# Second cross-attention with precomputed key maps, values as the stationary operand, and exponentials that take the maximum as their bias

## The chip, the cores and the metric

The kernel runs on one core of a Trainium2 chip. The time is device microseconds of one execution, median of three runs. The engines are TensorE (PE in the profile; its weight loads are PEld), VectorE (DVE), ScalarE (ACT), GpSimd (POOL) and SyncE (SP), each with its own instruction stream; they meet by semaphores.

## What is computed

Two layers, each a cross-attention with residual and a mixture-of-experts feed-forward with residual, over x of 8 images x 128 tokens x 128, all in float32. The context has 77 rows of 96 for each image. The change touches the second attention, which has 16 heads of 64:

```python
q = (layernorm(x) @ Wq).reshape(B, Nq, 16, 64)      # Wq 128 x 1024
k = (context @ Wk).reshape(B, Nk, 16, 64)           # Nk = 77
v = (context @ Wv).reshape(B, Nk, 16, 64)
attn = softmax(einsum('bqhd,bkhd->bhqk', q, k) / 8)
x = x + einsum('bhqk,bkhd->bqhd', attn, v).reshape(B, Nq, 1024) @ Wo + bo
```

Ahead of it stand the first attention (16 heads of 8) and the first expert layer (16 experts, 4 for each token); behind it the second expert layer (8 experts, one for each token).

## The kernel before

Each engine has a stream written out by hand, the order of which nothing alters. PSUM has eight banks, named S0 to S3, T0, T1, O and M. `plan_banks` writes down the order in which each bank is filled and emptied, and every user waits on the bank's `filled` or `freed` semaphore. An "image" below is one b of the eight. The stages in time are the first attention (to 109 us), routing and the first expert loop `fixed_units` (to 188), the second attention (`attention_1`, to 353), routing tables, and the second expert loop `units_1`.

In the second attention TensorE does for each image:
- `xT`: transposes the normalised tokens (ScalarE copies them to XT1);
- `q`: 8 matmuls of 128 columns give the queries of all heads, in two halves, copied to QT1 by ScalarE;
- `scores`: 16 matmuls of 77 columns on 64 rows each, two heads on two row halves;
- `probsT`: 16 transposes of the exponentials, four heads (a group g) in one bank; ScalarE copies them to PT;
- `pv`: 16 matmuls with the transposed exponentials stationary and the values moving, 65 columns each; the 65th column is of ones and gives the sum;
- `outT`: 8 transposes of the normalised result OS; ScalarE copies them to OT;
- `proj`: 8 matmuls of 128 columns, accumulated;
- `xnT`, `logits`, `rank`: the routing of an earlier image.

VectorE does for each group of four heads `shift` (maximum over the keys, then an addition that writes the shifted scores to SBUF) and `pv_out` (reciprocal of the sums, multiplication into OS). ScalarE's `exps` runs one exponential of 308 columns a group, in place. For each image VectorE has further `combine` (the sum of the four gathered expert rows and the statistics for the norm), `attn_norm`, `proj_out`, `normed`, and the small steps of the routing `choose`, `place` and `gate_out`. GpSimd gathers the expert rows of the first layer (`gather`, four indirect DMAs an image, three images ahead), raises variances to a power (`ln_pow` for the norm ahead of attention, `route_rstd` for the one ahead of routing), scatters routed tokens (`scatter`) and their row words (`meta`).

Keys K1 of the second layer are made during the first attention, all values V1 at the entry of the second (`v1`, 16 matmuls of 512 columns), 12 of them ahead of the first `xT`. SyncE loads the expert weights of the second layer into W, one expert after each image's scores.

## Time and profile before

| | us |
|---|---|
| median of 3 runs | 408.42 (405.4 to 409.94) |
| the profiled execution, its own time | 410.49 |
| its span, first to last instruction | 408.7 |
| TensorE busy | 353.8 (87%) |
| VectorE busy | 201.5 (49%) |
| ScalarE busy | 156.7 (38%) |
| GpSimd busy | 131.4 (32%) |
| mean granted clock of TensorE | 0.818 |

The span is the profiled execution's stretch from the first instruction to the last, 1.8 us less than that execution's time. Busy times count instructions that overlap once.
### The profile page before, as it was taken

How to read it: one execution, taken by the hardware profiler on the slowest of the kernel's cores; microseconds unless marked ns; L12 is line 12 of the kernel's file. 1: busy time of each engine (PE TensorE's matmuls, PEld its weight loads, DVE VectorE, ACT ScalarE, POOL GpSimd, SP SyncE). 2: the span in 40 equal slices, each digit the busy share in tenths (PEclk: the TensorE clock that was granted, in tenths of full speed). 3: DMA queues.
4: the chain of work that ended last, by engine and by line, in shares of the span. 5: the costliest groups of instructions: out<-in, count | busy, mean ns of one | idle time of the engine just before them, and what ended most of it. 6: DMA issues, size and time to landing. Idle time of an engine off the chain costs nothing.

```text
span 408.7 us, 8350 instructions
## 1 busy us (share of the span) xinstructions
PE 353.8 (87%) x2925; PEld 287.5 (70%) x2934; DVE 201.5 (49%) x697; ACT 156.7 (38%) x392; POOL 131.4 (32%) x192
## 2 busy tenths in 40 slices
PE   7789998998887799999987997969699999679990
PEld 4456675676664698985556996959599888549980
DVE  4455433443244566772268365535346663325760
ACT  1643202221243477666553343232215333015650
POOL 6314235423554000002764023412403203252441
PEclk9999558566586899998998599876859989559997
DMA  7999500000813567861132012120020210028711
GB/s 182 326 284 281 174 27 27 14 14 28 290 66 88 169 191 224 227 176 58 51 98 84 8 60 67 38 61 18 26 60 7 67 60 7 9 55 268 234 55 64
DMA packets 43545, 43.38 MB, mean 106 GB/s; under 512 B 6496, under 2 KB 39504, under 8 KB 43488
## 3 DMA queue, kind: packets, MB, share of 16 engines
q1 hardware_dynamic: 35488, 32.21, 27.3%
q0 software_dynamic: 3040, 5.74, 4.7%
q10 hardware_dynamic: 4976, 4.90, 3.7%
q8 instruction: 24, 0.39, 0.4%
q14 instruction: 17, 0.14, 0.1%
HBM read 26.29 MB, written 17.07 MB: 106 GB/s over the span
## 4 chain that ended last, share of the span: by engine, by line
PE 64%; issue 11%; DVE 5%; another core or an unknown queue 4%; SPq 4%; DMA 4%; ACT 4%; POOL 1%; POOLq 0%; ACTq 0%; DVEq 0%
PE bank_S L1949 6%; PE bank_M L1704 5%; PE bank_M L1678 4%; PE bank_O L1632 4%; PE bank_T L1661 3%; PE bank_S L1588 3%; PE bank_M L1742 3%; PE bank_S L1650 3%; PE bank_O L1678 3%; PE bank_O L1626 3%; PE bank_S L2003 3%; PE bank_S L1602 2%; PE bank_O L1958 2%; PE bank_M L1958 2%
## 5 line engine op out<-in xcount | busy, mean ns | idle before, releaser
L750 POOL DMA_INDIRECT dispatched<-XN,slot_u x40 | 40.2, 1004 | 22.5 <-DVE slot_u L1257 13.2
L758 POOL DMA_INDIRECT G<-expert_out,yslot x32 | 31.0, 969 | 19.5 <-DMA expert_out<-OS 10.6
L836 ACT ACTIVATE PT<-bank_T 77x512 f32<-77x512 f32 x40 | 23.0, 590 | 26.0 <-PE bank_T L1661 24.7
L734 POOL TENSOR_SCALAR var_eps<-row_data 128x1 f32<-128x1 f32 x8 | 1.8, 225 | 82.6 <-DVE row_data L1109 82.6
L836 ACT ACTIVATE QT<-bank_T 128x256 f32<-128x256 f32 (+2 forms) x47 | 16.5, 352 | 29.1 <-PE bank_T L1970 8.2
L879 ACT ACTIVATE scratch<-scratch 128x308 f32<-128x308 f32 x32 | 14.6, 457 | 30.5 <-DVE scratch L1169 27.0
L1678 PE MATMUL bank_M<-late,PT 77*128 77x65 f32 x112 | 18.1, 312 | 9.0 <-ACT QT L836 9.0
L1190 DVE RECIPROCAL RS<-bank_O 128x128 f32<-128x128 f32 x8 | 7.7, 957 | 34.1 <-PE bank_O L1632 18.2
L1704 PE MATMUL bank_M<-Wo_sb,OT 128*128 128x128 f32 x128 | 23.2, 356 | 0.8 <-ACT OT L836 0.8
L1678 PEld LDWEIGHTS bank_M<-late,PT 77*128 77x128 f32 x112 | 16.2, 223 | 10.6 <-ACT QT L836 9.7
L1163 DVE TENSOR_REDUCE negmax<-bank_S 128x4 f32<-128x308 f32 x32 | 15.1, 473 | 16.4 <-PE bank_S L1650 13.1
L1661 PE MATMUL bank_T<-C,scratch 128*77 128x128 f32 x128 | 22.5, 310 | 0.0
L1704 PEld LDWEIGHTS bank_M<-Wo_sb,OT 128*128 128x128 f32 x128 | 21.7, 264 | 1.0 <-issue 1.0
L1678 PE MATMUL bank_O<-late,PT 77*128 77x65 f32 x112 | 17.5, 307 | 4.5 <-DVE lg L1222 3.9
L820 POOL DMA_INDIRECT result<-OS,token x15 | 14.4, 957 | 19.0 <-DVE OS L1504 17.5
L1650 PE MATMUL bank_S<-K,QT 64*128 64x77 f32 x256 | 20.3, 306 | 0.0
L1678 PEld LDWEIGHTS bank_O<-late,PT 77*128 77x128 f32 x112 | 16.0, 221 | 5.9 <-DVE lg L1222 4.3
L836 ACT ACTIVATE QT<-bank_M 128x512 f32<-128x512 f32 x13 | 7.8, 597 | 30.7 <-remote 16.7
L1650 PEld LDWEIGHTS bank_S<-K,QT 64*128 64x128 f32 x256 | 17.9, 213 | 2.1 <-issue 0.8
L728 POOL TENSOR_SCALAR var_eps<-mv 128x1 f32<-128x1 f32 x8 | 2.1, 264 | 52.7 <-DVE mv L1109 52.7
L783 POOL TENSOR_TENSOR late<-late,C 128x1 f32<-128x1 f32 x15 | 3.1, 205 | 49.4 <-DMA late<-wp_dram 49.4
L1661 PEld LDWEIGHTS bank_T<-C,scratch 128*77 128x77 f32 x128 | 17.8, 175 | 1.1 <-issue 1.1
(286 smaller groups left out, 911.1 us busy)
## 6 DMA issues: line engine op xcount, KB each, us to landing
dispatched<-zeros SPq DMA_DIRECT2D x8, 1024.0 KB, 9.5
...
```

The costliest lines, as they stand in the source:

```text
L750: nc.gpsimd.indirect_dma_start(out=xs_dram, out_offset=bass.IndirectOffsetOnAxis(ap=slot_u[:, b, k:k + 1], axis=0), in_=XN[:, b, :], in_of ...
L758: nc.gpsimd.indirect_dma_start(out=G[:, b % 2, k, :], out_offset=None, in_=ys_dram, in_offset=bass.IndirectOffsetOnAxis(ap=yslot[:, b, k:k ...
L836: nc.scalar.activation(dst, src, func, **kw).then_inc(freed[bk], 1)
L879: nc.scalar.activation(pg, pg, ACT.Exp, scale=float(HD[1]) ** -0.5).then_inc(exp_done, 1)
L1163: link(nc.vector.tensor_reduce(negmax[:, g, :], sc, AX_X, ALU.max, negate=True))
L1632: ins = nc.tensor.matmul(bank["O"][32 * g:32 * g + 32, 128:256], C[0:M, C_SUM + 32 * j:C_SUM + 32 * j + 32], PT0[b % 2][:, g, 128 * j:128 ...
L1650: ins = nc.tensor.matmul(bank[f"S{g0 + k}"][:, M * j:M * j + M], QT1[r, b % 2, 2 * g0 + j, :], K1[r, 2 * g0 + j, M * b:M * b + M], start=T ...
L1661: ins = nc.tensor.transpose(o[0:M, 128 * j:128 * j + 128], P[:, b % 2, g, M * j:M * j + M], ident)
L1678: ins = nc.tensor.matmul(bank[bk][:, d * j:d * j + d], PT[:, g, 128 * j:128 * j + 128], V1[:, b, head_at(g, j), :], start=True, stop=True)
L1704: ins = nc.tensor.matmul(o[:, 0:128], OT[:, c, :], Wo_sb[:, c, :], start=(c == 0), stop=(c == 7))
L1949: nc.tensor.matmul(o[:, 0:256], weights_of(u)[:, 128 * half:128 * half + 128], xeT[:, r:r + 2, :], start=True, stop=True).then_inc(filled[ ...
L1958: ins = nc.tensor.matmul(o[:, 128 * m:128 * m + 128], hs[:, 2 * (u % RING) + m, :], weights_of(u)[:, 256:384], start=True, stop=True)
```

## The change

The scores of head h are X Wq_h K_h^T, so Wq_h K_h^T can be made without the tokens. `maps` does this at the entry: for 8 pairs of heads and two halves of four images, 32 matmuls of 308 columns on 64 rows each, into A1, which lies over W. `q` and its copies go; `scores` becomes 4 matmuls of 308 columns on all 128 rows. The factor 1/8 moves into the copies of K1.

`pv` has the values stationary (64 columns) and the transposed probabilities moving (128 columns); two heads write the two partition halves of a bank, which is already the form `proj` wants, so `outT`, OS and the 65th column go. Since the rows can't be scaled behind it any more, the probabilities are scaled ahead of the transposes: `scaled` on VectorE takes sums, reciprocal and product over 8 heads (616 columns). ScalarE's `exps` reads PSUM with the negative maximum as its bias, which makes 16 activations of 77 columns out of 4 of 308. VectorE's maxima are taken over 616 columns, two an image.

The order of all five streams is written anew: routing of an image stands one image later on VectorE, GpSimd's `ln_pow` stands between pairs of gathers, and the row words of the early images are sent near the end.

```diff
+        W = sb("W", [128, B * NH * M])
+        A1 = W[:].rearrange("p (b h m) -> p b h m", b=B, h=NH)
...
             ln_pow(0)
...
             gather(1, (2, 3))
-            gather(2)
+            gather(2, (0, 1))
             ln_pow(1)
-            for b in range(B - 1):
+            gather(2, (2, 3))
+            for b in range(B):
                 if b + 3 < B:
-                    gather(b + 3)
+                    gather(b + 3, (0, 1))
                 if b + 2 < B:
                     ln_pow(b + 2)
+                if b + 3 < B:
+                    gather(b + 3, (2, 3))
                 if 0 <= b - 1:
                     route_rstd(1, b - 1)
-                if 0 <= b - 2:
-                    scatter(1, b - 2)
...
+                if b == 6:
                     pool.wait_ge(meta_zeroed, 16)
-                if 0 <= b - 3:
-                    meta(b - 3)
-            route_rstd(1, B - 2)
+                    meta(0)
+                    meta(1)
...
             def exps(b, g):
-                act.wait_ge(freed[f"S{g}"], J(f"S{g}", "scores", 1, b, g))
-                pg = P[:, b % 2, g, :]
-                nc.scalar.activation(pg, pg, ACT.Exp, scale=float(HD[1]) ** -0.5).then_inc(exp_done, 1)
+                act.wait_ge(max_ready, 2 * b + g // 2 + 1)
+                tb = f"T{g % 2}"
+                if b >= 2:
+                    act.wait_ge(filled[tb], J(tb, "pT", 1, b - 2, g))
+                else:
+                    act.wait_ge(filled["O"], J("O", "u", 0, B - 1, 0))
+                for j in range(GH):
+                    ins = nc.scalar.activation(P[:, b % 2, g, M * j:M * j + M], bank[f"S{g}"][:, M * j:M * j + M], ACT.Exp,
+                                               bias=negmax[:, g, j:j + 1])
+                ins.then_inc(freed[f"S{g}"], 1)
...
+            def map_out(half):
+                for c in range(8):
+                    bk = map_bank(c, 0)
+                    copy_out(bk, J(bk, "map", half, c, 0), A1[:, 4 * half:4 * half + 4, 2 * c, :],
+                             bank[bk][:, 0:308].rearrange("p (b m) -> p b m", b=4))
...
+            def maxima_1(b, n):
+
+                if b > 0:
+                    for g in (2 * n, 2 * n + 1):
+                        dve.wait_ge(freed[f"S{g}"], J(f"S{g}", "scores", 1, b - 1, g))
+                for g in (2 * n, 2 * n + 1):
+                    dve.wait_ge(filled[f"S{g}"], J(f"S{g}", "scores", 1, b, g))
+                nc.vector.tensor_reduce(negmax[:, 2 * n:2 * n + 2, :],
+                                        bank_S[:, 2 * n:2 * n + 2, 0:GM].rearrange("p g (h m) -> p g h m", h=GH),
+                                        AX_X, ALU.max, negate=True).then_inc(max_ready, 1)
+
+            def scaled(b, n):
+
+                for g in (2 * n, 2 * n + 1):
+                    dve.wait_ge(freed[f"S{g}"], J(f"S{g}", "scores", 1, b, g))
+                pg = P[:, b % 2, 2 * n:2 * n + 2, :].rearrange("p g (h m) -> p (g h) m", h=GH)
+                link(nc.vector.tensor_reduce(psum[:, 2 * n:2 * n + 2, :].rearrange("p g h -> p (g h)"), pg, AX_X, ALU.add))
+                link(nc.vector.reciprocal(recip[:, 2 * n:2 * n + 2, :], psum[:, 2 * n:2 * n + 2, :]))
+                r = recip[:, 2 * n:2 * n + 2, :].rearrange("p g h -> p (g h)")
+                nc.vector.tensor_tensor(pg, pg, r[:, :, None].to_broadcast([128, 2 * GH, M]), ALU.mult).then_inc(p_ready, 1)
...
-                shift(0, 1)
+                maxima_1(0, 0)
+                maxima_1(0, 1)
+                v1_out(10)
                 combine(1)
...
+                scaled(0, 0)
+                v1_out(12)
...
+                maxima_1(1, 1)
+                scaled(1, 0)
+                for b in range(1, B):
+                    scaled(b, 1)
+                    if b + 1 < B:
+                        maxima_1(b + 1, 0)
+                    if 0 <= b - 3:
+                        choose(1, b - 3)
                     if b + 2 < B:
                         combine(b + 2)
-                    pv_out(b, 0)
-                    shift(b + 1, 0)
-                    shift(b + 1, 1)
-                    pv_out(b, 1)
-                    shift(b + 1, 2)
-                    pv_out(b, 2)
+                    proj_out(1, b - 1)
+                    if b + 1 < B:
+                        maxima_1(b + 1, 1)
                     if 0 <= b - 3:
...
+                        place(1, b - 3)
                     if b + 2 < B:
                         attn_norm(b + 2)
...
+                    if b + 1 < B:
+                        scaled(b + 1, 0)
+                    normed(1, b - 1)
+                    if 0 <= b - 4:
+                        gate_out(b - 4, b - 3)
...
             dve.wait_ge(ld_c, LD_C)
+            map_out(0)
+            v1_out(1)
+            v1_out(3)
+            map_out(1)
+            v1_out(5)
+            v1_out(7)
+            v1_out(9)
             combine(0)
             attn_norm(0)
...
+            def maps(half):
...
+                for c in range(8):
+                    for k in range(2):
+                        bk = map_bank(c, k)
+                        o = use(bk, J(bk, "map", half, c, k))
+                        r = slice(64 * k, 64 * k + 64)
+                        nc.tensor.matmul(o[:, 0:308], Wq_sb[r, c, :], K1[r, c, 308 * half:308 * half + 308],
+                                         start=True, stop=True).then_inc(filled[bk], 1)
...
+            def scores(b, n):
+                if n == 0:
+                    pe.wait_ge(freed["T0"], J("T0", "xT", b))
...
+                for g in (2 * n, 2 * n + 1):
+                    o = use(f"S{g}", J(f"S{g}", "scores", 1, b, g))
+                    nc.tensor.matmul(o[:, 0:GM], XT1[:], A1[:, b, GH * g:GH * g + GH, :], start=True, stop=True)\
+                        .then_inc(filled[f"S{g}"], 1)
...
-                pe.wait_ge(exp_done, NG * b + g + 1)
+                pe.wait_ge(p_ready, 2 * b + g // 2 + 1)
...
+            def pv(b, n):
+                bk, number = product("pv", 1, b, n)
                 o = use(bk, number)
+                for m in (2 * b, 2 * b + 1):
+                    pe.wait_ge(freed[v1_bank(m)], J(v1_bank(m), "v1", m))
...
+                    pe.wait_ge(freed[f"T{g % 2}"], J(f"T{g % 2}", "pT", 1, b, g))
                 for c in range(4):
...
+                    for k in range(2):
+                        h = 8 * n + 2 * c + k
+                        j = h % GH
+                        ins = nc.tensor.matmul(o[64 * k:64 * k + 64, 128 * c:128 * c + 128], V1[:, b, h, :],
+                                               PT[:, h // GH, 128 * j:128 * j + 128], start=True, stop=True)
                 ins.then_inc(filled[bk], 1)
...
+                maps(0)
+                v1(0, 4)
+                maps(1)
+                v1(4, 6)
+                xT(0)
+                scores(0, 0)
+                scores(0, 1)
+                v1(10, 4)
...
                 probsT(0, 0)
...
+                for b in range(1, B):
+                    if b + 1 < B:
+                        scores(b + 1, 0)
                     probsT(b, 0)
-                    xT(b + 1)
                     probsT(b, 1)
-                    if last:
-                        outT(b - 1, 0)
-                    q(b + 1, 0)
+                    proj(1, b - 1)
                     pv(b, 0)
-                    scores(b + 1, (0, 1))
-                    q(b + 1, 1)
+                    if b + 1 < B:
+                        scores(b + 1, 1)
+                    if 0 <= b - 3:
+                        rank(1, b - 3)
                     probsT(b, 2)
-                    if last:
-                        outT(b - 1, 1)
+                    probsT(b, 3)
+                    if 0 <= b - 2:
+                        xnT(1, b - 2)
+                    if b + 2 < B:
+                        xT(b + 2)
                     pv(b, 1)
-                    probsT(b, 3)
-                    if routed:
-                        xnT(1, b - 2)
-                    scores(b + 1, (2, 3))
-                    pv(b, 2)
-                    if routed:
+                    if 0 <= b - 2:
                         logits(1, b - 2)
```

The maps at the entry. TensorE, from the last matmuls of `fixed_units`, before (L1912 and L1958 are the expert loop's, L2003 is `v1`, L1734 `xT`, L1742 `q`, L1650 `scores`):

```order
L1912 MATMUL bank_T<-b_sb,OT 128x128 x4
L1958 MATMUL bank_O<-late,OS 128x128 x2
L2003 MATMUL bank_S<-Wv_sb,ctx_sb 77x512 x12
L1734 MATMUL bank_M<-C,XA 128x128
L1742 MATMUL bank_M<-XT,Wq_sb 128x128 x4
L1742 MATMUL bank_O<-XT,Wq_sb 128x128 x4
L1650 MATMUL bank_S<-K,QT 128x77 x16
```

and now (L1630 is `maps`, L1946 `v1`, L1709 `xT`, L1642 `scores`):

```order
L1901 MATMUL bank_O<-late,OS 128x128 x2
L1630 MATMUL bank_S<-K,Wq_sb 128x308 x16
L1946 MATMUL bank_T<-Wv_sb,ctx_sb 77x512 x2
L1946 MATMUL bank_O<-Wv_sb,ctx_sb 77x512
L1946 MATMUL bank_M<-Wv_sb,ctx_sb 77x512
L1630 MATMUL bank_S<-K,Wq_sb 128x308 x16
L1946 MATMUL bank_T<-Wv_sb,ctx_sb 77x512 x2
L1946 MATMUL bank_O<-Wv_sb,ctx_sb 77x512
L1946 MATMUL bank_M<-Wv_sb,ctx_sb 77x512
L1946 MATMUL bank_T<-Wv_sb,ctx_sb 77x512 x2
L1709 MATMUL bank_T<-C,XA 128x128
L1642 MATMUL bank_S<-W,XT 128x308 x4
```

The first `xT` stood behind 12 value matmuls and stands behind 32 maps and 10 value matmuls.

One image of the loop on TensorE, before, from its first `probsT` (L1661; L1690 is `outT`, L1678 `pv`):

```order
L1661 MATMUL bank_T<-C,scratch 77x128 x4
L1734 MATMUL bank_M<-C,XA 128x128
L1661 MATMUL bank_T<-C,scratch 77x128 x4
L1690 MATMUL bank_O<-C,OS 128x128 x4
L1742 MATMUL bank_M<-XT,Wq_sb 128x128 x4
L1678 MATMUL bank_O<-late,PT 128x65 x4
L1650 MATMUL bank_S<-K,QT 128x77 x8
L1742 MATMUL bank_M<-XT,Wq_sb 128x128 x4
L1661 MATMUL bank_T<-C,scratch 77x128 x4
L1690 MATMUL bank_O<-C,OS 128x128 x4
L1678 MATMUL bank_M<-late,PT 128x65 x4
L1661 MATMUL bank_T<-C,scratch 77x128 x4
```

and now the whole of an image (L1650 is `probsT`, L1679 `proj`, L1664 `pv`, L1702 and L1703 `rank`, L1686 `xnT`, L1693 `logits`):

```order
L1642 MATMUL bank_S<-W,XT 128x308 x2
L1650 MATMUL bank_T<-C,scratch 77x128 x8
L1679 MATMUL bank_M<-Wo_sb,OT 128x128 x8
L1664 MATMUL bank_O<-PT,late 64x128 x8
L1642 MATMUL bank_S<-W,XT 128x308 x2
L1702 MATMUL bank_O<-hot,C 128x8
L1703 MATMUL bank_O<-mcum,C 128x8
L1650 MATMUL bank_T<-C,scratch 77x128 x8
L1686 MATMUL bank_O<-C,XN 128x128
L1709 MATMUL bank_T<-C,XA 128x128
L1664 MATMUL bank_M<-PT,late 64x128 x8
L1693 MATMUL bank_O<-Wr_sb,XNT 128x8
```

Queries and `outT` are gone, scores are 4 matmuls, and `rank` stands ahead of the second pair of transposes.

VectorE in an image, before, from `combine`'s last rows (L1179 and L1185 are `pv_out`, L1163 and L1169 `shift`, L1264 and L1265 `gate_out`):

```order
L1109 BN_AGGR mv<-st 128x2
L1282 TENSOR_TENSOR XB<-X,bo_sb 128x128
L1179 RECIPROCAL recip<-bank_O 128x4
L1185 TENSOR_TENSOR OS<-bank_O,recip 128x256
L1163 TENSOR_REDUCE negmax<-bank_S 128x4
L1169 TENSOR_TENSOR scratch<-bank_S,negmax 128x308
L1163 TENSOR_REDUCE negmax<-bank_S 128x4
L1169 TENSOR_TENSOR scratch<-bank_S,negmax 128x308
L1179 RECIPROCAL recip<-bank_M 128x4
L1185 TENSOR_TENSOR OS<-bank_M,recip 128x256
L1163 TENSOR_REDUCE negmax<-bank_S 128x4
L1169 TENSOR_TENSOR scratch<-bank_S,negmax 128x308
```

and now (L1194, L1096 and L1097 are `proj_out`, L1153 `maxima_1`, L1245 and L1249 `place`, L1278 `attn_norm`, L1162, L1163 and L1165 `scaled`, L1201 `normed`):

```order
L1194 TENSOR_TENSOR XR<-bank_M,XB 128x128
L1096 BN_STATS st<-XR 128x6
L1097 BN_AGGR row_data<-st 128x2
L1153 TENSOR_REDUCE negmax<-bank_S 128x8
L1245 TENSOR_TENSOR prod<-hot,bank_O 128x8
L1249 TENSOR_REDUCE slot_u<-prod 128x1
L1278 TENSOR_SCALAR XA<-X,mv,rstd 128x128
L1162 TENSOR_REDUCE psum<-scratch 128x8
L1163 RECIPROCAL recip<-psum 128x8
L1165 TENSOR_TENSOR scratch<-scratch,recip 128x616
L1201 TENSOR_SCALAR XN<-XR,row_data 128x128
L1256 TENSOR_REDUCE vsum<-vexp 128x1
```

The four additions and four products on PSUM have made way for two products on SBUF, and `scaled` of the next image now stands between `attn_norm` and `normed`.

## Rows read from the trace of the kernel before

**Rows 1.** Stretches: us, busy us of PE, PEld, DVE, ACT, POOL, PEclk, DMA share, GB/s.

```profile
41.00:96.00 55.00, 51.46 (x592) 35.89 (x595) 21.61 (x72) 11.99 (x28) 21.23 (x30) 0.62 0.16 51
223.60:241.20 17.60, 17.60 (x118) 17.11 (x119) 8.01 (x24) 6.06 (x12) 1.48 (x3) 0.66 0.13 42
241.20:259.20 18.00, 15.20 (x131) 14.23 (x129) 10.67 (x37) 6.42 (x15) 5.68 (x8) 0.91 0.17 50
259.20:282.00 22.80, 19.14 (x129) 17.99 (x130) 10.68 (x40) 6.35 (x15) 6.69 (x9) 0.72 0.14 40
282.00:306.80 24.80, 20.16 (x130) 19.15 (x131) 11.11 (x40) 6.45 (x15) 7.67 (x10) 0.71 0.14 39
306.80:321.60 14.80, 13.89 (x130) 13.09 (x131) 10.37 (x39) 6.35 (x15) 3.83 (x6) 0.98 0.15 46
```

**Rows 2.** Timeline of ScalarE in the image 282 to 307.

```profile
292.50 0.60 ACT L836 ACTIVATE QT<-bank_M 128x512 f32<-128x512 f32 x1 [6.54 <-remote]
```

**Rows 3.** Timeline of GpSimd, same image.

```profile
282.79 0.73 POOL L735 TENSOR_TENSOR row_data<-var_eps,C 128x2 f32<-128x2 f32 x1
...
283.70 1.10 POOL L750 DMA_INDIRECT dispatched<-XN,slot_u  x1 [0.18 <-issue]
...
287.69 0.95 POOL L758 DMA_INDIRECT G<-expert_out,yslot  x1 [0.30 <-issue]
...
291.50 0.57 POOL L710 TENSOR_TENSOR rstd<-var_eps,C 128x1 f32<-128x1 f32 x1
```

**Rows 4.** Timeline of TensorE, one image at the full clock: start, us, line, operation.

```profile
308.61 1.13 PE L1742 MATMUL bank_M<-XT,Wq_sb 128*128 128x128 f32 x8
309.57 1.02 PE L1678 MATMUL bank_O<-late,PT 77*128 77x65 f32 x8
310.52 1.12 PE L1650 MATMUL bank_S<-K,QT 64*128 64x77 f32 x16
...
312.56 0.60 PE L1661 MATMUL bank_T<-C,scratch 128*77 128x128 f32 x4
313.00 0.60 PE L1690 MATMUL bank_O<-C,OS 128*128 128x128 f32 x4
...
319.23 2.00 PE L1704 MATMUL bank_M<-Wo_sb,OT 128*128 128x128 f32 x16
321.07 0.29 PE L1727 MATMUL bank_O<-hot,C 128*128 128x8 f32 x2
```

**Rows 5.** Timeline of TensorE, entry of the second attention.

```profile
187.88 12.16 PE L2003 MATMUL bank_S<-Wv_sb,ctx_sb 96*77 96x512 f32 x24
200.03 0.30 PE L1734 MATMUL bank_M<-C,XA 128*128 128x128 f32 x1
```

**Rows 6.** Timeline of TensorE, first attention: matmuls in 32-row and 32-column tiles.

```profile
16.11 0.79 PE L1588 MATMUL bank_S<-W 32*128 32x308 f32 x4
...
22.71 1.08 PE L1626 MATMUL bank_O<-PT,W 77*32 77x128 f32 x32
```

**Rows 7.** Groups of VectorE instructions, shapes apart, 188 to 354 us (the first: whole span).

```profile
L1154 DVE TENSOR_REDUCE NM<-bank_S 128x8 f32<-128x616 f32 x16 | 12.7, 793 | 10.8 <-PE bank_S L1588 10.8
...
L1169 DVE TENSOR_TENSOR scratch<-bank_S,negmax 128x308 f32<-128x308 f32 x32 | 15.3, 478 | 1.1
...
L1163 DVE TENSOR_REDUCE negmax<-bank_S 128x4 f32<-128x308 f32 x32 | 15.1, 473 | 16.4 <-PE bank_S L1650 13.1 <-remote 3.2
...
L1275 DVE SCALAR_TENSOR_TENSOR X<-G,gates,X 128x128 f32<-128x128 f32 x24 | 8.6, 360 | 3.4 <-DMA G<-expert_out,yslot 2.6
...
L1185 DVE TENSOR_TENSOR OS<-bank_O,recip 128x256 f32<-128x256 f32 x14 | 5.9, 424 | 0.5
```

**Rows 8.** Groups of ScalarE instructions, shapes apart, whole span.

```profile
L879 ACT ACTIVATE scratch<-scratch 128x308 f32<-128x308 f32 x32 | 14.6, 457 | 30.5 <-DVE scratch L1169 27.0 <-issue 3.5
...
L1076 ACT ACTIVATE scratch<-bank_S,W 128x128 f32<-128x128 f32 x16 | 5.0, 366 | 1.0 <-PE bank_S L1980 1.0
```

**Rows 9.** The chain that ended last: start, us, what.

```profile
349.00 3.77 PE bank_M L1704 x16
```

408 lines of the change are left out of this document (132 added, 276 removed), and 3 rows, old and new, of the table LAST.

## The prediction, on record before the changed kernel ran

> **What bounds the kernel now.** I first cut the span into stages. The second attention takes 188 to 352.8 us, 165 of 408.7, and only this stage is edited; the ends of its images are the starts of their first transposes. The view of busy time by stretch [rows 1] shows TensorE busy for 13.9 of 14.8 us in the one image that ran almost wholly at the full clock (0.98), with VectorE at 10.4, ScalarE at 6.4 and GpSimd at 3.8. TensorE bounds that image. The four images ahead of it took 17.6, 18.0, 22.8 and 24.8 us. Two things separate them from 14.8: a granted clock of 0.66, 0.91, 0.72 and 0.71, and a wait in three of them, of which the longest is shown: ScalarE's copy of the second half of the queries stood 6.54 us for something that the profile can't name [rows 2], with GpSimd's four gathers in progress beside it [rows 3], and TensorE then stood for that copy. In the two images from 259.2 to 306.8 the clock of 0.715 means 1.2 GHz for 57% of the time.
>
> **TensorE's work for an image, at the full clock.** Starts in the timeline give 0.96 us for 4 matmuls of q, 0.95 for 4 of pv, 1.1 for 8 of the scores (two on two row halves), 0.44 for 4 transposes, 1.84 for proj [rows 4]. Before: q 1.9, pv 3.8, scores 2.2, probsT 1.8, outT 0.9, proj 1.8, the rest 0.8: 13.2, which agrees with 13.9 busy. Removed: q 1.9 and outT 0.9. The new scores are 4 matmuls of 308 columns. The v1 matmuls of 512 columns took 12.16 us for 12, part of it at the low clock [rows 5], so 308 columns cost at most 0.61; I take 0.55, 2.2 in all, the same as before. The new pv is 16 matmuls of 128 columns in pairs of column halves. Without overlap it costs 16 x 0.24 = 3.8. The first attention ran 16 matmuls of 128 columns, four side by side, in 1.08 [rows 6]; two side by side should take twice that less the tail, 2.0, which I take, since it is the nearest row. Sum after: 2.2 + 2.0 + 1.8 + 1.8 + 0.8 = 8.6, a saving of 4.6.
>
> That pairs of column tiles run together is what the first attention's row shows. The Trainium skill, "TensorE: Matmul & The Clock Gate", Part 3, says that a weight load overlaps with running matmuls only where the row group differs. Both heads of a pair use the same rows, so by that rule pv would lie nearer 3.8 and the image nearer 10.4. The row speaks against it, having equal rows too.
>
> **VectorE's work for an image.** Before: four maxima of 0.473, four additions of 0.478, four times a reciprocal (0.18, estimated from its short form) and a product of 0.424 [rows 7]: 6.2. After: two maxima over 616 columns at 0.793, a shape that the first attention has; two sums over 616 columns in SBUF, which no row shows, taken as 0.79; two reciprocals; two products over 616. An addition grew by nothing I can see, but the maximum grew by 0.32 from 308 to 616 columns, so the product is 0.478 + 0.32 = 0.80. That makes 2 x 0.79 + 2 x (0.79 + 0.18 + 0.80) = 5.1. The bounds for the sum and the product are 0.6 and 0.96 (no fixed part; twice the short form). VectorE's busy time goes from 10.4 to 9.3 and, with 0.1 for each of nine hand-overs, fills about 10.2.
>
> **ScalarE and GpSimd.** The two copies of q go, 1.2 us. Four exponentials of 0.457 become 16 of 77 columns; the nearest row is 128 columns from PSUM with a bias at 0.366 [rows 8], overlapped by a tenth, so about 0.23 each in a sequence and 3.7 in all. ScalarE rises from 6.4 to about 7.1, hidden beneath VectorE. GpSimd does for an image four gathers of 0.95 plus 0.30, a power of 0.8 in all, one of 0.95 and a scatter of 1.4 [rows 3]: 8.3.
>
> **The loop.** With TensorE at 8.6 the order of VectorE and GpSimd decides. I walk one image from the start of `scaled(b, 1)`: scaled to 1.8, maxima 2.6, choose 3.6, combine 5.8, proj_out 6.5, maxima 7.2, place and attn_norm 7.9, scaled 9.7. `normed(b - 1)` needs `route_rstd`, which GpSimd reaches only behind two gathers that its new order puts ahead of it: ln_pow ends at 6.5, gathers at 9.0, route_rstd at 10.1. Normed and gate_out end at 10.8. TensorE fits in: `xT(b + 2)` waits for attn_norm to 7.9, behind it pv and logits end at 9.3, and its own gaps are 0.5 and 1.4 us. I add 0.7, as the clean image before needed 14.8 for 13.2 of work: **11.5 us an image at the full clock**. At 1.2 GHz TensorE's work doubles to 17.2 and bounds again: 17.5.
>
> Which clock? The images with gathers had 43% full and 57% half. At this division the new loop does 0.43/11.5 + 0.57/17.5 images a us, 14.3 each, 14.5 with a remnant of the unnamed wait. I take that for images 1 to 4, 11.5 for 5 and 10.5 for 6, which have no gathers: 80 us.
>
> **The entry.** Here the change costs. Before, TensorE ran 12 values from 187.88 and `xT(0)` at 200.03 [rows 5], when the first gathered rows had just come. Now 16 pairs of maps stand ahead. A pair of 308-column matmuls took 0.79 with its tail in 32-row tiles [rows 6]; between 0.55 and 0.79 I take 0.67, since each pair waits for two copies: 10.7 us. Unpaired they would be 17.6. With 10 values at 0.86 (an estimate: the 1.01 above, less the part at the low clock) and 2 us for the low clock and for ScalarE's table load, TensorE is through at about 209. VectorE's copies of maps and values stand ahead of `combine(0)`, so combine (four products of 0.36 and the statistics, 2.0), the power 0.8, the norm and the transpose follow: `xT(0)` at about 213, 13 us later. TensorE idles 4 us there, and I expect the low clock behind it, as the stretch from 223.6 had with 0.66 [rows 1]. GpSimd's `ln_pow(0)` waits too, and behind it the gathers of images 1 and 2. The scores, values 10 to 15, and softmaxes of images 0 and 1 follow at this clock, and `scaled(1, 1)` starts at about 236, where the loop before began at 223.6: a loss of 12.4.
>
> **The end.** Behind the start of image 7's `scaled(7, 1)` come transposes, copies, pv, copy and proj, 9 us. Before, proj of the last image ended at 352.8 [rows 9]. Now: 236 + 80 + 9 = 325, a gain of 27.8. The rest, 56 us of routing, tables and second expert loop, keeps its work; the expert weights, which SyncE loads after each image's scores, have ample time. The span becomes 380.9, the profiled time 382.7 by the 1.8 around the span, and the median, which lay 2.1 below the profiled run, **380.6**.
>
> **Rivals.**
> *The clock holds.* TensorE's new gaps are short, and the clean image had gaps too and kept 0.98. If entry and loop run at the full clock, the loop starts at 231 and takes 5 x 11.5 + 10.5 = 68: proj ends at 308, and the time is 363.5. For it: q, whose copy stood, is gone. Against: gathers remain in the same images.
> *The clock stays mostly low.* In the first attention, with tiled matmuls and TensorE busy for 51.5 of 55 us, the clock was 0.62, so low for 76% [rows 1], and the new pv is tiled. Then an image costs 1/(0.24/11.5 + 0.76/17.5) = 15.6, the loop 94, the time 395.
> *Slower.* If TensorE, now idle for a quarter of each image, never gets the full clock in this stage, every image takes 17.5 (105 for six), and the wait beside the gathers returns with 3 us in each of four images (12); with an entry to 238 and an end of 13 at that clock, 238 + 105 + 12 + 13 = 368 against 352.8, and the time is 424. It decides from 15.5 us an image in the mean upward with a wait on top. Against it: the clean image's clock with TensorE idle for 0.9.
> *The pairs don't run together.* Then maps cost 7 more and each image 1.8 at the full and 3.6 at the low clock, of which VectorE hides the first: 20 in all, 400.
> The product reads two SBUF tensors. By the Trainium skill, "SBUF — State Buffer", "SBUF: two separate sides", such an instruction and a GpSimd instruction that reads SBUF block each other. In this kernel that means `scaled` against the powers, at worst 0.57 or 0.73 [rows 3] for each of 14 products: up to 9 us, 390. Combine's products read two SBUF tensors as well and average 0.36 for 128 columns while gathers run, so I give it 5 in 100, within the range.
>
> **Chances.** Forecast 0.45, clock holds 0.2, mostly low 0.18, unpaired 0.05, port 0.05, slower 0.05, within 1% 0.02. The range runs from 363 to 397: the full clock at one end, the mostly low one at the other. Of these cases, faster by over 1% (about what a measurement of this kernel tells from no change) has 0.93, within it 0.03, slower 0.04.
>
> **What the changed profile would show.** Entry: maps in about 11 us, `xT(0)` near 213 and TensorE idle ahead of it. Loop: TensorE busy about 8.6 for an image at the full clock, pv at 1.0 for 8 matmuls, VectorE at 9 to 10 and busiest; `normed` waiting for GpSimd. The clock row tells the first three cases apart. I'd be wrong if exponentials of 77 columns cost over 0.45, which would make ScalarE the bound, or if `xT(0)` came earlier than 208.

## The result and the profile after

| | before | after |
|---|---|---|
| median, 4 runs each | 407.13 us (405.4 to 409.94) | 368.1 us (365.39 to 374.67) |
| ratio | | 0.901 (0.892 to 0.910) |
| profiled execution, its own time | 410.49 | 374.67 |
| its span | 408.7 | 372.9 |
| TensorE, VectorE, ScalarE, GpSimd busy | 353.8, 201.5, 156.7, 131.4 | 321.1, 204.8, 167.2, 133.9 |
| mean granted clock | 0.818 | 0.826 |

Some executions of either kernel are a few per cent slower at a lower granted clock; the ratios leave these out, the medians don't. The profiled execution of after was the slowest of its four, 6.6 us above the median. Its stages, in the view of busy time by stretch (columns as in [rows 1]; the first stretch is from the first maps to the first `proj`, the second from there to the last `proj`, the third the tail behind it):

```profile
191.10:244.60 53.50, 42.98 (x176) 23.19 (x176) 29.63 (x65) 25.57 (x70) 20.01 (x24) 0.86 0.16 48
244.60:315.50 70.90, 63.12 (x535) 52.54 (x533) 55.45 (x176) 46.36 (x155) 35.37 (x46) 0.96 0.23 69
...
319.30:372.90 53.60, 36.13 (x281) 32.94 (x281) 26.05 (x122) 18.80 (x62) 21.23 (x23) 0.82 0.43 129
```

The last `proj` ends at 319.3 where before it ended at 352.8 [rows 9]. The images of the loop, by the starts of their `proj`:

```profile
254.40:263.60 9.20, 8.67 (x78) 7.24 (x77) 7.92 (x20) 7.11 (x25) 5.03 (x8) 1.00 0.30 90
263.60:274.40 10.80, 9.61 (x83) 7.67 (x81) 9.32 (x30) 7.35 (x26) 6.63 (x9) 1.00 0.27 79
274.40:286.50 12.10, 10.93 (x82) 8.70 (x81) 10.51 (x34) 7.69 (x26) 7.96 (x10) 0.89 0.29 83
286.50:296.50 10.00, 9.58 (x83) 8.13 (x82) 9.16 (x32) 6.93 (x26) 2.84 (x5) 0.97 0.22 68
```

The clock column is what sets these apart from [rows 1]: the first three, with gathers, ran at 1.00, 1.00 and 0.89, where before had 0.91, 0.72 and 0.71. TensorE is idle for 0.4 to 1.2 us in each, and neither it nor VectorE nor ScalarE has a wait over 1.5 us (GpSimd, which has less to do, waits up to 4.9).

TensorE's timeline, entry, then parts of one image, then the last `proj` (in brackets the idle time before, and its releaser):

```profile
193.94 4.05 PE L1630 MATMUL bank_S<-K,Wq_sb 64*128 64x308 f32 x24 [1.50 <-ACT W L819]
201.51 5.41 PE L1630 MATMUL bank_S<-K,Wq_sb 64*128 64x308 f32 x32
216.42 0.44 PE L1709 MATMUL bank_T<-C,XA 128*128 128x128 f32 x1 [4.20 <-DVE XA L1278]
217.24 4.47 PE L1642 MATMUL bank_S<-W,XT 128*128 128x308 f32 x8 [0.37 <-ACT XT L819]
...
270.33 0.33 PE L1686 MATMUL bank_O<-C,XN 128*128 128x128 f32 x1 [0.89 <-DVE prod L1245]
...
271.14 1.09 PE L1664 MATMUL bank_M<-PT,late 77*64 77x128 f32 x16
...
272.40 1.28 PE L1642 MATMUL bank_S<-W,XT 128*128 128x308 f32 x4
...
315.49 3.76 PE L1679 MATMUL bank_M<-Wo_sb,OT 128*128 128x128 f32 x16
```

Sixteen maps take 5.41. TensorE then stands 4.20 for VectorE's `attn_norm`, and the four scores behind that wait take 4.47, where the pair at 272.40 takes 1.28: here the half clock follows the idle time. It doesn't always: in image 274.4 to 286.5 it sets in at about 283, where TensorE's longest idle time just before was 0.88. Eight matmuls of `pv` take 1.03 between starts.

The groups of VectorE and ScalarE (shapes apart, second attention) have the new softmax:

```profile
L1165 DVE TENSOR_TENSOR scratch<-scratch,recip 128x616 f32<-128x616 f32 x16 | 12.9, 804 | 0.5
L1153 DVE TENSOR_REDUCE negmax<-bank_S 128x8 f32<-128x616 f32 x16 | 12.7, 797 | 13.2 <-PE bank_S L1642 13.2
L1162 DVE TENSOR_REDUCE psum<-scratch 128x8 f32<-128x616 f32 x16 | 12.6, 790 | 1.7 <-issue 1.1 <-ACT scratch L867 0.6
...
L1163 DVE RECIPROCAL recip<-psum 128x8 f32<-128x8 f32 x16 | 3.2, 203 | 0.5
```

```profile
L867 ACT ACTIVATE scratch<-bank_S,negmax 128x77 f32<-128x77 f32 x128 | 29.5, 343 | 8.3 <-DVE negmax L1153 4.8 <-issue 3.5
```

An exponential by itself reads 343 ns, but 128 of them fill only 29.5 us, 0.23 each, since they overlap.

The chain that ended last, in image 263.6 to 274.4, is no longer TensorE's. It runs along VectorE from a sum through combine to GpSimd and back by `normed`:

```profile
262.92 0.80 DVE psum L1162
...
268.90 0.57 POOL rstd L690
...
269.65 1.08 POOL G L738
...
271.04 0.95 POOL G L738
272.01 0.58 POOL var_eps L714
...
272.67 0.74 POOL row_data L715
...
273.70 0.80 DVE psum L1162
```

From sum to sum, 262.92 to 273.70, it is 10.8 us.

### The profile page after: what moved, and what is told of

It is laid out like the page before. It is cut to its first block, busy times and chain, and to the rows that moved or that the text cites. A ratio compares the mean times of both kernels' runs of the same rounds, so it can differ in the third digit from the quotient of the medians.

```text
span 372.9 us, 7737 instructions
## 1 busy us (share of the span) xinstructions
PE 321.1 (86%) x2614; PEld 242.9 (65%) x2614; DVE 204.8 (55%) x655; ACT 167.2 (45%) x482; POOL 133.9 (36%) x191
## 4 chain that ended last, share of the span: by engine, by line
PE 68%; DVE 10%; issue 7%; DMA 4%; POOL 4%; ACT 2%; SPq 2%; POOLq 0%; another core or an unknown queue 0%; ACTq 0%; DVEq 0%
PE bank_S L1892 7%; PE bank_S L1642 4%; PE bank_O L1614 4%; PE bank_S L1570 4%; PE bank_S L1923 3%; PE bank_O L1608 3%; PE bank_S L1584 3%; PE bank_M L1679 3%; PE bank_T L1650 3%; PE bank_S L1630 3%; PE bank_O L1901 2%; PE bank_S L1717 2%; PE bank_S L1594 2%; PE bank_M L1901 2%; DVE X L1267 2%
## 5 line engine op out<-in xcount | busy, mean ns | idle before, releaser
L730 POOL DMA_INDIRECT dispatched<-XN,slot_u x40 | 40.3, 1007 | 23.3 <-DVE slot_u L1249 14.6
L867 ACT ACTIVATE scratch<-bank_S,negmax 128x77 f32<-128x77 f32 x128 | 29.5, 343 | 8.3 <-DVE negmax L1153 4.8
L1642 PE MATMUL bank_S<-W,XT 128*128 128x308 f32 x64 | 23.4, 496 | 2.7 <-ACT XT L819 2.7
L1650 PE MATMUL bank_T<-C,scratch 128*77 128x128 f32 x128 | 19.6, 303 | 2.1 <-DVE scratch L1165 2.1
L1650 PEld LDWEIGHTS bank_T<-C,scratch 128*77 128x77 f32 x128 | 16.9, 166 | 5.0 <-issue 3.9
L1153 DVE TENSOR_REDUCE negmax<-bank_S 128x8 f32<-128x616 f32 x16 | 12.7, 797 | 13.2 <-PE bank_S L1642 13.2
L1142 DVE TENSOR_REDUCE NM<-bank_S 128x8 f32<-128x616 f32 x16 | 12.7, 795 | 10.8 <-PE bank_S L1570 10.8
L1679 PE MATMUL bank_M<-Wo_sb,OT 128*128 128x128 f32 x128 | 18.5, 306 | 0.1
L1679 PEld LDWEIGHTS bank_M<-Wo_sb,OT 128*128 128x128 f32 x128 | 17.8, 223 | 0.3 <-ACT OT L819 0.3
L689 POOL TENSOR_SCALAR var_eps<-mv 128x1 f32<-128x1 f32 (+1 forms) x10 | 2.3, 229 | 43.8 <-DVE mv L1097 43.8
L1892 PE MATMUL bank_S<-QT,W 128*128 128x256 f32 x64 | 17.7, 402 | 0.0
L1642 PEld LDWEIGHTS bank_S<-W,XT 128*128 128x128 f32 x64 | 12.4, 214 | 7.8 <-ACT XT L819 3.4
L1570 PE MATMUL bank_S<-W 32*128 32x308 f32 x64 | 15.1, 551 | 1.6 <-DVE W L1129 0.8
L1878 PE MATMUL bank_T<-C,QT 128*128 128x128 f32 x62 | 12.5, 290 | 4.0 <-DMA QT<-dispatched 3.7
L1892 PE MATMUL bank_S<-QT,late 128*128 128x256 f32 x60 | 15.6, 382 | 0.0
```

Of the source, the lines that this page charges most:

```text
L730: nc.gpsimd.indirect_dma_start(out=xs_dram, out_offset=bass.IndirectOffsetOnAxis(ap=slot_u[:, b, k:k + 1], axis=0), in_=XN[:, b, :], in_of ...
L867: ins = nc.scalar.activation(P[:, b % 2, g, M * j:M * j + M], bank[f"S{g}"][:, M * j:M * j + M], ACT.Exp, bias=negmax[:, g, j:j + 1])
L1570: ins = nc.tensor.matmul(bank[f"S{g % 2}"][:, 0:GM], QT0[r, T * b:T * b + T], KX0[r, :, M * b:M * b + M], start=True, stop=True)
L1642: nc.tensor.matmul(o[:, 0:GM], XT1[:], A1[:, b, GH * g:GH * g + GH, :], start=True, stop=True)\
L1650: ins = nc.tensor.transpose(o[0:M, 128 * j:128 * j + 128], P[:, b % 2, g, M * j:M * j + M], ident)
L1679: ins = nc.tensor.matmul(o[:, 0:128], OT[:, c, :], Wo_sb[:, c, :], start=(c == 0), stop=(c == 7))
```

## Experiments

The experiments ran on different chips, and these turned out to differ: the kernel before took 353.5 to 354.9 us on two chips and 414.7 on another. So a kernel is compared by its ratio to before on its own chip, and with the changed kernel only where that ran on the same chip or on one where before was as quick.

| kernel | median us | before beside it | ratio (95%) |
|---|---|---|---|
| c_after | 370.85 | 414.68 | 0.896 (0.887 to 0.904) |
| c_before | 424.74 (one execution) | 414.68 | none |
| e5_unpaired | 378.78 | 414.68 | 0.913 (0.903 to 0.923) |
| e8_all_three | 365.22 | 414.68 | 0.881 (0.873 to 0.890) |
| c2_after | 335.12 | 354.31 | 0.945 (0.935 to 0.954) |
| f1_before_no_q_no_outT | 350.0 | 354.31 | 0.986 (0.976 to 0.995) |
| d3_double_matmuls | 362.15 | 354.89 | 1.024 (1.014 to 1.033) |
| d4_before_no_q | 351.85 | 354.89 | 0.997 (0.992 to 1.003) |
| e1_route_early | 334.77 | 353.47 | 0.945 (0.937 to 0.954) |
| e2_combine_early | 330.62 | 353.47 | 0.935 (no interval) |
| e3_double_matmuls | 363.67 | 353.47 | 1.035 (1.027 to 1.043) |
| e4_before_no_q | 357.58 | 353.47 | 0.999 (0.992 to 1.007) |

### The changed kernel and the one before, on two more chips

> The changed kernel again, beside the kernel before on the chip of this call. On the chip of the first experiments the kernel before took 353.5 us where it took 408 to 407 on the chip of the first comparison, with the first attention at the full clock. Theory A (what the change saves is TensorE's work, at whatever clock the chip grants): the ratio to before stays near 0.90 to 0.95, its images take 9.5 to 11 us, and the absolute gain shrinks to 15 to 25 us where the clock is granted anyway. Rival B (the gain of 39 us was mostly the clock's): the ratio comes above 0.97.

> The kernel before again, for its profile on this chip. Theory A: images take 14 to 15 us at the full clock, TensorE busy 13 to 14 of them, and the waits of ScalarE for something unnamed beside the gathers are there as well, since they don't come from the clock. Rival B: the waits are missing where the clock is high.

> The changed kernel once more, beside the kernel before. The chips fall in two kinds: before takes 407 to 415 us on one, with unnamed waits and long stretches of half clock, and 353 to 355 on the other, with neither. On the second kind the changed kernel has not run. Theory A (its gain is TensorE's removed work, some 3 to 4 us an image at the full clock, less the longer entry): 336 to 340 us, ratio 0.95 to 0.96. Rival B (the gain on the first kind was mostly waits and clock): 345 us or more, ratio above 0.97. On the first kind: 0.90 again.

The gain is 43.8 us on the chip where before took 414.7 and 19.2 where it took 354.3, ratios of 0.896 and 0.945. What the chips differ in stands in the view of waits: first before on the slower chip, then after on the quicker one (41 to 109, and 41 to 90 us; engine and what waited, releaser, sum, times, longest). Lines of `c_before`:

```profile
ACT XNT L836 <- remote: 19.1, 4, 6.0
DVE RS L1190 <- remote: 15.8, 3, 5.4
```

and of `c2_after`:

```profile
DVE RS L1182 <- PE bank_O L1614: 8.4, 5, 2.4
```

"Remote" is a wait the profile can't name. None of the eight traces taken on the quicker chips has one, not even those of the old kernel with instructions left out. On the slower chip the first attention, the same in both kernels, has it in `c_after` as well; the difference is in the second attention. Windows of `c_before` (from the first `proj` to the last, and the tail):

```profile
245.20:359.70 114.50, 99.79 (x740) 94.15 (x739) 57.38 (x212) 36.92 (x85) 30.86 (x43) 0.80 0.13 37
...
363.50:422.90 59.40, 39.72 (x286) 36.17 (x286) 25.99 (x124) 18.50 (x63) 22.29 (x24) 0.79 0.39 117
```

and of `c_after`:

```profile
242.20:312.20 70.00, 61.97 (x534) 51.38 (x533) 56.18 (x177) 46.51 (x155) 35.59 (x46) 0.96 0.24 70
...
316.00:370.00 54.00, 35.68 (x281) 32.94 (x281) 25.71 (x122) 18.29 (x62) 21.16 (x23) 0.82 0.42 128
```

The loop lost 44.5 us. Counted in full-clock time it went from 114.5 x 0.80 = 91.6 to 70.0 x 0.96 = 67.2: by this estimate some 24 us are less time in any clock, some 20 are the clock. `c_before` is a single execution of 424.7 us, 10 above the median of before on that chip, so 44.5 is on the high side. The two traces of the first comparison (239.3 to 349.0 at 0.84, and 70.9 at 0.96) give 38.8 us, of which again 24 are less time in any clock and 15 are the clock. On the quicker chip `c2_after` needs 71.7 for the same stretch at 0.96, so the changed kernel's loop runs alike on both, and what the chips differ in fell on the old one. So theory A holds for the quicker chip (336 to 340 and 0.95 to 0.96 expected, 335.1 and 0.945 measured, a little more than that), and on the slower one its "15 to 25 where the clock is granted" has about as much again on top. What makes that second half, the waits or the clock, no experiment on such a chip has taken apart.

Before's three long waits of this stage are there again in `c_before`, as its theory A has it (one image at the full clock took 14.47 us with TensorE busy for 13.57, as it has it too). But the clock is low on that chip, so its rival B (missing where the clock is high) was not put to the test; the eight traces of the quicker chips fit B. The waits stand at the copy of the queries; beside them, GpSimd's last gather of the image and its power. `c_before`, timeline of ScalarE:

```profile
256.92 0.60 ACT L836 ACTIVATE QT<-bank_M 128x512 f32<-128x512 f32 x1 [4.71 <-remote]
...
278.84 0.60 ACT L836 ACTIVATE QT<-bank_M 128x512 f32<-128x512 f32 x1 [5.76 <-remote]
...
303.04 0.60 ACT L836 ACTIVATE QT<-bank_M 128x512 f32<-128x512 f32 x1 [6.27 <-remote]
```

and of GpSimd:

```profile
254.97 0.94 POOL L758 DMA_INDIRECT G<-expert_out,yslot  x1 [0.30 <-issue]
...
276.73 0.94 POOL L758 DMA_INDIRECT G<-expert_out,yslot  x1 [0.30 <-issue]
...
301.52 0.94 POOL L758 DMA_INDIRECT G<-expert_out,yslot  x1 [0.30 <-issue]
```

Each wait ends 0.6 to 1.2 us behind the last of four gathers in a row. The changed kernel issues two, a power, and two, and its loop has no such wait over 1.3 us. Whether the split or the missing queries did that was not tried on such a chip.

### TensorE's work put back

```diff
+                    nc.tensor.matmul(o[:, 0:GM], XT1[:], A1[:, b, GH * g:GH * g + GH, :], start=True, stop=True)
                     nc.tensor.matmul(o[:, 0:GM], XT1[:], A1[:, b, GH * g:GH * g + GH, :], start=True, stop=True)\
                         .then_inc(filled[f"S{g}"], 1)
...
-                for c in range(4):
+                for c in (0, 1, 2, 3, 0, 1, 2, 3):
                     for k in range(2):
```

> The changed kernel with each matmul of scores and of pv issued twice into the same place, which gives TensorE 4.3 us of work an image back (2.3 and 2.0 at the full clock), about what the change took away (4.6). Theory A (the gain is TensorE's removed work): images take 13.5 to 15 us at the full clock, the time rises by 25 to 40 us, to 393 to 408. Rival B (the gain is the new order, the removed copy of the queries with its unnamed wait, and VectorE's shorter work; TensorE's work was no more than half of it): the time rises by less than 20 us. The granted clock of the loop tells more: if TensorE's load by itself brings the half clock, it falls from 0.95 to the 0.7 to 0.9 of before.

> The kernel with scores and pv issued twice, again. On the chip of its first run the trace has no wait for something unnamed on any engine and the first attention ran at 0.86 to 1.0; on the chips where before takes 407 to 415, each of before's three longest waits for something unnamed in this stage stands at ScalarE's copy of the queries and is followed by some 12 us of half clock, and the changed kernel has none there. Theory A (TensorE's load brings the waits and the half clock): with 4.3 us an image back, both return, images take 17 us or more in the mean, and the time is at or above 410. Rival B (they hung on the queries, their order and their copy): images take 13 to 14.5 us with a clock over 0.9, and the time is 25 to 32 us above the changed kernel, near 0.96 of before. If the chip is again one without such waits, it can only repeat the first run: 1.03 of before.

Both landed on quick chips, at 1.035 and 1.024 of before, 27 us above `c2_after` for `d3` on the same chip and 28.5 for `e3` on the other. The executions of `e3` lie far apart, 354.9 to 366.4 us, 1.004 to 1.037 of the median before, so its sign is surer than its size. One image of each at the full clock, `d3_double_matmuls`:

```profile
251.30:265.00 13.70, 12.99 (x123) 11.01 (x122) 9.59 (x32) 7.16 (x26) 4.91 (x7) 1.00 0.20 59
```

and the same image of `c2_after`:

```profile
236.10:246.90 10.80, 9.63 (x83) 7.69 (x82) 9.28 (x32) 7.36 (x26) 7.62 (x10) 1.00 0.31 87
```

TensorE has 3.4 us more and the image is 2.9 longer. With its work put back, the new kernel is no quicker than the old one, a little slower (it keeps its longer entry). Theory A is right in this direction, rival B (under 20 us) is out. The clock stayed at 0.97 over the doubled loop of `d3` (211.9 to 303), so on such a chip the load alone does not bring the half clock. On the slower kind it was not tried.

### TensorE's work taken out of the old order

```diff
-                    q(b + 1, 0)
...
-                    q(b + 1, 1)
...
-                    q_out(b + 1, 0)
-                    q_out(b + 1, 1)
```

> The kernel before, with the queries made for images 0 and 1 only; the later images use those again, so q and its copies are left out of six images (TensorE 1.9 us an image, ScalarE 1.2). Theory A (ScalarE's waits of 4.8 to 6.5 us for something unnamed hang on the copy of the queries): they go with it, and the half clock that follows TensorE's idle time goes too: 6 x 1.9 plus 9 for the waits plus some clock, 20 to 30 us less than before. Rival B (the waits are of TensorE's signals while GpSimd issues gathers, whoever waits): another copy of ScalarE's takes the wait over, and the time falls by 8 to 14 us only.

> The kernel before with the queries of images 0 and 1 only, again. On a chip with the unnamed waits. Theory A (the waits hang on the copy of the queries): they are gone, and the time falls by 20 to 30 us. Rival B (TensorE's signals come late there, whoever waits): another copy of ScalarE's or a maximum of VectorE's waits 3 to 6 us in the same images, and the time falls by less than 14 us. On a chip without these waits: 1.00 of before, as in the first run.

Ratios 0.999 and 0.997: neither theory's gain came, A's 20 to 30 us nor B's 8 to 14 (`d4` was expected to give 1.00 on such a chip). Both runs were on chips where no trace has the waits that A is about (before itself was not profiled there), so A on the waits stays untested. One image at the full clock, first of before (on the slower chip, but at clock 1.00 too), then the same one of `d4_before_no_q`:

```profile
319.23:333.69 14.46, 13.56 (x130) 12.76 (x130) 8.71 (x33) 6.35 (x15) 2.99 (x4) 1.00 0.16 49
```

```profile
266.59:279.99 13.40, 11.62 (x115) 10.90 (x114) 8.72 (x33) 5.28 (x13) 3.00 (x4) 1.00 0.16 52
```

Of 1.9 us less work 1.1 came through. The rest stands in TensorE's timeline, in every image, where the queries had been the cover for a round trip; the wait for `lg` was there before as well (0.89 at 318.29 in before):

```profile
257.91 1.11 PE L1674 MATMUL bank_O<-late,PT 77*128 77x65 f32 x8 [0.89 <-ACT OT L834]
...
265.65 1.10 PE L1674 MATMUL bank_O<-late,PT 77*128 77x65 f32 x8 [0.89 <-DVE lg L1218]
```

The 1.1 us an image, some 6 in all, are not in the total. The granted clock tells where they can have gone: over the executions that the ratios count, its mean was 0.891 to 0.909 in `d4` and `e4` and 0.901 to 0.929 in before beside them. In this trace the half clock is in the entry (0.77 from 152 to 209.7, against 0.92 in `c2_after` from 154 to 206) and in the first two images. Since no profile of before exists on these chips, where before had less of it is open.

> The kernel before with neither the queries nor outT and their copies from image 2 and image 1 on; the later images use those of image 0 and 1 again, so that projections and scores are of stale data. It takes from TensorE 2.8 us an image, most of what the change takes, in the old order. Without the queries alone nothing was gained (1.00 and 0.997), since TensorE then stood for outT's copy and for VectorE's lg. Theory A (outT with its copy was what the order then hung on): now 10 to 18 us come off on a chip without unnamed waits. Rival B (the old order hangs on VectorE's chain of shift, pv_out and routing, and only the new order turns TensorE's saving into time): less than 6 us. On a chip with unnamed waits, whether ScalarE or VectorE still has one tells if they hang on the queries' copy.

```diff
-                    if last:
-                        outT(b - 1, 0)
+                    if b == 1:
+                        outT(0, 0)
```

(and so for the other half, its copies, and the last two images). It gives 0.986 (0.976 to 0.995), 4.3 us, inside rival B's bound of 6. One image of it, and the `proj` at its start:

```profile
251.40:265.20 13.80, 12.43 (x107) 11.68 (x106) 10.40 (x40) 4.38 (x11) 3.82 (x6) 0.88 0.18 58
```

```profile
251.41 3.09 PE L1692 MATMUL bank_M<-Wo_sb,OT 128*128 128x128 f32 x16
```

TensorE is idle for 1.4 of it, and its clock is 0.88. All five whole images of this loop have a clock of 0.83 to 0.88, and in each the `proj` at its start takes 3.1 to 3.7 us where it took 2.00 at the full clock [rows 4]. At 0.88 some 3.3 us of the image are at the half clock, which costs up to 1.65: an estimate of 12.1 us at the full clock, against 14.46 in before. So rival B has the number, but its reason is not shown. The order let most of the 2.8 us through, and a half clock in every image took a good part of it back; the mean clock of its four executions was 0.881 to 0.886, that of before beside them 0.901 to 0.919. Why the clock falls there, with no idle time over 0.89 ahead of it in this image, is open.

Together with the doubling: the smaller work of TensorE is needed for the gain. In the old order it was not enough for it, partly for TensorE's waits (the 0.89 in `d4`) and partly for the clock. Whether the new order as such was needed, or only a loop that keeps the full clock, these runs don't tell.

### Pairs of column halves

```diff
-                for c in range(4):
-                    for k in range(2):
+                for k in range(2):
+                    for c in range(4):
```

> The changed kernel with pv's eight matmuls of a half issued four on the first column half and then four on the second, instead of alternating; the same work and result. Theory A (two column halves side by side run together, so that 8 matmuls take 1.03): alternation is lost, 8 take 1.8 to 1.95, TensorE gets 1.6 us more for each image, and the time rises by 2 to 8 us over the changed kernel. Rival B (the pairs don't run together, and 1.03 is what 64 columns of weights cost anyway): nothing changes.

`e5_unpaired`, timeline of TensorE:

```profile
268.79 1.58 PE L1664 MATMUL bank_O<-PT,late 77*64 77x128 f32 x16
270.30 1.30 PE L1642 MATMUL bank_S<-W,XT 128*128 128x308 f32 x4
```

Eight take 1.51 between starts, against 1.03 alternating: 1.0 for an image, and 7.9 us over `c_after` on the same chip. Theory A's sign and total are right, its 1.8 to 1.95 too high: eight full-width matmuls of as many columns take 1.92 (0.96 for four of `q` [rows 4]), so even unpaired ones are cheaper than that, and whether by their 64 columns of weights or by some overlap is not shown. Alternating the column halves, with equal rows, is worth 0.48 of 1.51.

### The chain through GpSimd, the entry, the end

```diff
+                if 0 <= b - 1:
+                    route_rstd(1, b - 1)
                 if b + 3 < B:
                     gather(b + 3, (2, 3))
-                if 0 <= b - 1:
-                    route_rstd(1, b - 1)
```

> The changed kernel with GpSimd's route_rstd of an image ahead of the second pair of gathers instead of behind it. Theory A (the order of VectorE and GpSimd sets the pitch of the images that have gathers): in the changed kernel's trace normed stood for route_rstd, which stood behind two gathers of 2.5 us together, and images 3 and 4 took 10.8 and 11.0 us at a clock near 1. With route_rstd early they take 9.3 to 9.8 us, and the time falls by 3 to 6 us (ratio to the changed kernel 0.985 to 0.992). Rival B (TensorE's own work sets the pitch): TensorE was busy for 9.6 of 10.8 us there; the images stay at 10.5 or more and the time within 1 us.

0.945, the same as `c2_after`, which ran on another chip; with intervals of about 0.009 on each, a difference under some 4 us would not show in the times, so the trace has to decide. The wait of `normed` is gone, and another took its place 0.3 us earlier. `e1_route_early`, the chain that ended last in the image that answers to the one shown of after:

```profile
236.76 0.31 PE bank_T L1709
...
238.16 1.01 ACT scratch L867 x4
239.26 0.81 DVE psum L1162
```

Sum to sum is 10.46 here (228.80 to 239.26), against 10.78 in after. Behind GpSimd stands the loop xT, XT copy, exponentials, sum. Theory A failed: the image had two chains of nearly one length. Rival B has the result, but not its reason: the chain has 0.31 us of TensorE in it.

```diff
             map_out(1)
+            combine(0)
             v1_out(5)
             v1_out(7)
-            v1_out(9)
-            combine(0)
             attn_norm(0)
+            v1_out(9)
```

> The changed kernel with VectorE's combine(0) ahead of its last three copies of values in the entry, and attn_norm(0) ahead of the last. Theory A (the entry is lost to VectorE's copies, which stand ahead of combine(0)): TensorE's idle time of 4.2 us ahead of the first xT goes, xT(0) starts 4 us earlier, and the stretch of half clock behind it goes or shrinks: 4 to 8 us less. Rival B (the gathered rows or a bank come late anyway): TensorE waits elsewhere in the entry and the time falls by less than 1.5 us.

`e2_combine_early`, timeline of TensorE, last values, xT(0), scores:

```profile
175.00 1.88 PE L1946 MATMUL bank_T<-Wv_sb,ctx_sb 96*77 96x512 f32 x4
176.72 0.32 PE L1709 MATMUL bank_T<-C,XA 128*128 128x128 f32 x1
177.40 2.34 PE L1642 MATMUL bank_S<-W,XT 128*128 128x308 f32 x8 [0.37 <-ACT XT L819]
```

The idle 4.2 us are gone and the scores run at the full clock, 2.34 for what took 4.47 in both after and `c2_after`. That shows the half clock in this place to hang on the idle time. From the first map (155.8) to the first `proj` (197.9) it is 42.1 us, against 49.8 in `c2_after` and 53.5 in after. That is theory A: 7.7 us less by the trace, where it expected 4 to 8. The times say it less clearly: the median, 330.6, is 4.5 us below the 335.1 of `c2_after`, but the four executions fall in two pairs, 324.2 and 325.6, and 335.6 and 337.3, so there is no interval. The trace is of the quickest.

> The changed kernel with route_rstd ahead of the second pair of gathers, combine(0) and attn_norm(0) ahead of the last copies of the entry, and TensorE's proj of the last image ahead of rank(5). If the three prices are independent: 2 to 5 us from the images with gathers, 4 to 6 from the entry, 1 to 2 from the end, 7 to 12 us less than the changed kernel. Rival: the clock takes it back, or TensorE's own work bounds the images: under 5 us.

```diff
-                rank(1, B - 3)
                 proj(1, B - 1)
+                rank(1, B - 3)
                 logits(1, B - 2)
```

(with the two edits above). 365.22 against 370.85 on the same chip, 5.6 us less: below the 7 to 12 of three independent prices, above the rival's 5. The entry shows where some may have gone. xT(0) no longer waits, but this profile's maps fell into a stretch of half clock ahead of the edit (5.80 for the 24 records that take 4.05 in `c_after`), and another stood over the transposes after it:

```profile
224.00 1.96 PE L1650 MATMUL bank_T<-C,scratch 128*77 128x128 f32 x8 [2.11 <-DVE scratch L1165]
```

It is the quickest version on its chip (363.1 to 370.2, against 369.5 to 371.8 for the changed kernel).

## Why the prediction held, point by point

The forecast was 380.6, the result 368.1, inside 363 to 397. The likeliest case was not the one that came: the rival "the clock holds", at 363.5, is nearer in number and in the loop; the entry, with its idle time and half clock, went by the forecast. That the number is within 13 us owes something to errors that cancel, below.

- **The step that failed** is "which clock": "The images with gathers had 43% full and 57% half. At this division the new loop does [...] 14.3 each". Images took 10.1 us in the mean (70.9 for seven), at 0.96. The old division belonged to the old loop, not to the stage: on the slower chips its waits of 4.7 to 6.5 us ran ahead of stretches of half clock, and the new loop has no such wait and only a few microseconds of half clock, at 283. Whether the waits brought the half clock is not shown. On quick chips the changed loop has the same 0.96.
- **The image at the full clock**: 11.5 forecast, 10.8 measured with routing, 9.2 without. The walk itself came out: from the start of `scaled`, `route_rstd` ended at 10.1 in it and at 10.5 in the trace. The 0.7 added by hand was wrong, and image 2 has no `choose`.
- **TensorE's sum**: 8.6 forecast with routing, 9.6 busy with it (8.67 without), so 1.0 short, as the 13.2 for before was 0.7 short of 13.9. `pv` 2.0 forecast, 2 x 1.03 measured; scores 2.2, 2 x 1.12.
- **VectorE and ScalarE**: product 0.80 and 0.804, sum 0.79 and 0.790, reciprocal 0.18 and 0.203, exponential 0.23 and 0.23, VectorE 9.3 and 9.32, ScalarE 7.1 and 7.1 to 7.4.
- **The entry**: a pair of maps at 0.67, measured 5.41 / 8 = 0.68. `xT(0)` 25.1 us behind the end of the expert loop, measured 25.3; TensorE idle 4 there, measured 4.20, with the half clock behind it. `scaled(1, 1)` came 51.5 behind that end instead of 48.1. The stage itself began 3.2 later, since the stages ahead of it had less clock in the profiled execution (0.78 against 0.81).
- **The end** was mis-sized: 9 forecast from `scaled(7, 1)` to the end of `proj`, measured 319.3 - 304.7 = 14.6. I had not counted that `rank(5)` stands ahead of that `proj` and waits for `choose(5)` (1.14 idle), and `proj` ran at the half clock, 3.76 for 1.9. With the `rank` at the half clock these are some 4 of the 5.6; beside them stand shorter waits for copies (0.36, 0.75 and 0.77).
- **The sum of the errors**: +3.2 start, +3.4 entry, -18.0 loop (62.0 for 80), +5.6 end, -2.3 tail (53.6 for 55.9) make -8.1, which is 380.9 to 372.9, the span. The loop alone was 18 us too long, and the other errors hid over half of that. The remaining 4.5 us of the 12.5 between 380.6 and 368.1 are no part of the trace: the forecast put the median 2.1 below the profiled execution, and it lay 6.6 below.
- **Slower, unpaired** did not come. Unpaired was a right worry of wrong size: 7.9 us for `pv`, where the forecast had 13 for it (20 with the maps, which stayed paired in the run).
- **The page on the clock gate.** The Trainium skill, "TensorE: Matmul & The Clock Gate", Part 3, lets a weight load overlap with running matmuls only where the row group differs; with equal row groups `pv` would by the prediction's estimate take 1.9 for 8. The runs show 1.03 alternating and 1.51 not, so the measurement decides against that rule here. The table of measured speedups in the same Part, with 2.38x for three column tiles, points the same way as the runs.
- **The port.** VectorE's product did not grow (0.804 in the mean). GpSimd did. `after`, GpSimd's timeline, once beside the product of 271.71 and once beside none:

```profile
272.01 0.57 POOL L714 TENSOR_SCALAR var_eps<-row_data 128x1 f32<-128x1 f32 x1
...
291.32 0.22 POOL L714 TENSOR_SCALAR var_eps<-row_data 128x1 f32<-128x1 f32 x1
```

```profile
271.71 0.80 DVE L1165 TENSOR_TENSOR scratch<-scratch,recip 128x616 f32<-128x616 f32 x1
```

The 0.22 step became 0.57 and ended 0.07 behind the product. That is what "SBUF: two separate sides" on the Trainium skill's page "SBUF — State Buffer" would have; it cost 0.35 in each of two images of the loop (272.0 and 282.8), not the 9 us of the rival. No run took the port apart from other causes.

That the removed work makes the gain was argued in the prediction; the doubling shows it in the new order, on quick chips. The runs without `q` and `outT` show that in the old order its removal gave little in the total, for waits and for a lower clock. On the slower kind of chip, where the forecast was made and the gain is twice as large, neither was run. That the waits for something unnamed hang on the queries' copy, or on four gathers in a row, is not shown.
